# Cross attention: the sums of one key tile in eight go to an accumulator of their own, by an accumulating DMA

## What is computed

```
q = query @ Wq.T + bq; k = key @ Wk.T + bk; v = value @ Wv.T + bv      # 16 heads of 32
att = jnp.einsum('bhqd,bhkd->bhqk', q, k) / jnp.sqrt(jnp.float32(D_K))
att = jnp.where(mask == 0, -jnp.inf, att)
scores = jax.nn.softmax(att, axis=-1)
out = jnp.einsum('bhqk,bhkd->bhqd', scores, v)
```

## Time and profile before

| | us |
|---|---|
| median of 3 runs (3172.49 to 3174.4) | 3174.29 |
| the profiled execution, its own time | 3177.68 |
| its span, first to last instruction | 3175.9 |
| PE busy, all stages | 3039.1 (96%) |
| DVE busy | 1824.3 (57%) |
| ACT busy | 1346.5 (42%) |
| POOL busy | 43.9 (1%) |

### The profile page before, as it was taken

One profiled execution on the slowest core, in us unless ns is written; L12 is line 12 of the kernel. 1 busy time (PEld: TensorE's weight loads), 2 busy tenths in 40 slices (PEclk: granted clock), 3 DMA queues, 4 the chain that ended last, 5 costly groups with the idle time before them and its releaser, 6 DMA issues. The chain is left out here.

```text
span 3175.9 us, 45035 instructions
## 1 busy us (share of the span) xinstructions
PE 3039.1 (96%) x15853; PEld 1820.8 (57%) x15853; DVE 1824.3 (57%) x1578; ACT 1346.5 (42%) x1871; POOL 43.9 (1%) x38
## 2 busy tenths in 40 slices
PE   8999999998999999999999997979799899999998
PEld 4888888886333333333333333358344688888886
DVE  4444444444999999999999996047244111111111
ACT  3212121222988888888888882135100011111110
POOL 0000000000000000000000000000000200000000
PEclk9999999999999999999999998976899999999999
DMA  5555555555554555544554541000330678788774
GB/s 194 185 186 191 186 193 183 197 183 181 124 132 121 126 120 124 130 121 118 122 130 120 131 120 57 0 5 1 123 159 17 226 301 314 303 311 310 303 305 179
DMA packets 231254, 518.54 MB, mean 163 GB/s; under 512 B 20578, under 2 KB 86626, under 8 KB 201436
## 3 DMA queue, kind: packets, MB, share of 16 engines
q1 hardware_dynamic: 227564, 508.74, 49.7%
q0 software_dynamic: 3584, 8.39, 1.2%
HBM read 403.62 MB, written 113.44 MB: 163 GB/s over the span
## 5 line engine op out<-in xcount | busy, mean ns | idle before, releaser
L791 DVE TENSOR_TENSOR AC<-AC,PR 128x2048 f32<-128x2048 f32 x496 | 1093.5, 2278 | 7.2 <-ACT PR L754 7.2
L754 ACT ACTIVATE PR<-PS 128x1024 f32<-128x1024 f32 x1024 | 994.4, 1023 | 144.5 <-DVE AC L791 98.2
L665 PE MATMUL PS<-QS,KS 128*128 128x512 f32 x2048 | 645.0, 436 | 19.2 <-ACTq L763 9.0
L665 PEld LDWEIGHTS PS<-QS,KS 128*128 128x128 f32 x2048 | 321.0, 189 | 549.9 <-ACT PR L754 514.4
L712 PE MATMUL PS<-PR,VC 128*32 128x512 f32 x4096 | 547.3, 606 | 1.0 <-ACT PR L754 1.0
L1393 ACT ACTIVATE SE<-PS,GB 128x128 f32<-128x128 f32 x256 | 73.2, 368 | 630.7 <-PE PS L1349 630.7
L365 ACT ACTIVATE KH<-PS,bk_s 128x512 fp32r<-128x512 f32 x128 | 88.1, 688 | 561.4 <-PE PS L416 561.4
L276 DVE SCALAR_TENSOR_TENSOR KL<-PS,bk_s,KH 128x512 fp32r<-128x512 f32 x128 | 95.8, 750 | 274.6 <-ACT KH L365 274.6
L1349 PEld LDWEIGHTS PS<-XE,WG 128*128 128x128 f32 x2048 | 238.8, 193 | 23.7 <-issue 23.7
L1349 PE MATMUL PS<-XE,WG 128*128 128x128 f32 x2048 | 240.5, 276 | 0.8 <-issue 0.8
L1349 PE MATMUL PS<-XE,WU 128*128 128x128 f32 x2048 | 239.1, 275 | 0.0
(11 more groups left out here) (149 smaller groups left out, 2265.9 us busy)
## 6 DMA issues: line engine op xcount, KB each, us to landing
KS<-kh_d SPq DMA_DIRECT2D x256, 256.0 KB
WU<-in_up_w SPq DMA_DIRECT2D x64, 1024.0 KB, 4.8
WG<-in_gw SPq DMA_DIRECT2D x64, 1024.0 KB, 6.9
WD<-in_down_w SPq DMA_DIRECT2D x64, 1024.0 KB, 8.9
AT<-in_ctx SPq DMA_DIRECT2D x32, 1024.0 KB, 5.5
kh_d<-KH SPq DMA_DIRECT2D x32, 1024.0 KB, 4.4
kl_d<-KL SPq DMA_DIRECT2D x32, 1024.0 KB, 6.4
v_d<-VS SPq DMA_DIRECT2D x128, 256.0 KB, 3.0
```

The costliest lines, as they stand in the source:

```text
L665: m = pe.matmul(PS[:, 2 * slot + jj, :], KS[s][:, j, t * P:(t + 1) * P], QS[x_][:, j, :], start=True, stop=True)
L754: nc.scalar.activation(PR[t][:, 2 * hp:2 * hp + 2], PS[:, 2 * slot:2 * slot + 2, :], ACT.Exp, scale=SCALE).then_inc(s_exp, 1)
L791: v.tensor_tensor(a[:], a[:], PR[t][:], ALU.add).then_inc(s_acc, 1)
```

## The change

The tile `q = KT - 1` of a pair (first chunk, `t = 3`, buffer PR3) is no longer added by DVE. POOL issues a DMA from PR3 to a new accumulator `AP[x_]`: a plain copy in a group's first pair, and in the other seven a DMA with `accum_op=ALU.add`, which adds the 1 MB in PR3 to the 1 MB in AP. It waits for both exponentials of the tile, and for the DMA of the pair before. DVE skips the tile (its counts `ADDS` fall from 8 to 7 a pair); where `normal` stood behind that tile's add it stands in its place. ACT waits for the DMA, in place of DVE's sum, before it writes PR3 again in the pair's second chunk. PE's denominator reads three accumulators in place of two, 12 matmuls for 8. `s_step` is counted up and waited for by nobody.

```diff
--- before.py
+++ after.py
@@ -579,13 +579,14 @@
 
 
         s_wo = sem("output_weights_in")
-        s_s, s_exp, s_pv, s_acc, s_l, s_o, s_rec, s_norm = (sem(n) for n in (
-            "scores_ready", "exp_ready", "tile_values_added", "sums_added",
+        s_s, s_exp, s_pv, s_acc, s_pacc, s_step, s_l, s_o, s_rec, s_norm = (sem(n) for n in (
+            "scores_ready", "exp_ready", "tile_values_added", "sums_added", "dma_sums_added", "dma_sums_step",
             "denominator_ready", "output_copied", "reciprocal_ready", "output_normal"))
         UN = 2 * KT
         GU = NCH * UN
         GT = NCH * KT
-        ADDS = 2 * KT
+        PQ = KT - 1
+        ADDS = 2 * KT - 1
         KVB, QSB = 4 * 16, 4 * 16
         SLOTS, PAIRS = 3, NCH // 2
         GA = PAIRS * ADDS
@@ -600,6 +601,7 @@
             VC.append(sb("VC1", [P, KT, P]))
             PR = [sb(f"PR{i}", [P, J, SQ]) for i in range(KT)]
             AC = [[sb(f"AC{x}{h}", [P, J, SQ]) for h in range(2)] for x in range(2)]
+            AP = [sb(f"AP{x}", [P, J, SQ]) for x in range(2)]
             RC = sb("RC", [P, SQ])
 
             def all_groups(engine, group):
@@ -656,6 +658,23 @@
                 nc.gpsimd.memset(KS[1][3 * DH:P].bitcast(F32), 1.0).then_inc(s_row, 1)
                 nc.gpsimd.memset(QS[1][3 * DH:P].bitcast(F32), 0.0).then_inc(s_row, 1)
 
+                def group(bg, x_, rounds, head=False, tail=False):
+                    def pair(i, phase, first=False, last=False):
+                        pool.wait_ge(s_exp, (bg * NCH + i * 2) * UN + 2 * PQ + 1 + SLOTS + 1)
+                        if first:
+                            if not head:
+                                pool.wait_ge(s_norm, bg)
+                            pool.sem_inc(s_step, 1)
+                            nc.gpsimd.dma_start(AP[x_][:], PR[PQ][:]).then_inc(s_pacc, 16)
+                        else:
+                            pool.wait_ge(s_pacc, (bg * PAIRS + i) * 16)
+                            pool.sem_inc(s_step, 1)
+                            nc.gpsimd.dma_start(AP[x_][:], PR[PQ][:], accum_op=ALU.add).then_inc(s_pacc, 16)
+
+                    all_pairs(pool, pair)
+
+                all_groups(pool, group)
+
             @block.tensor
             def _(pe):
                 def scores(u, s, x_, slot):
@@ -674,9 +693,9 @@
                 def denominator(x_):
 
                     for j in range(J):
-                        for h in range(2):
-                            m = pe.matmul(PS[j * DH:(j + 1) * DH, SUMB, :], ones[:], AC[x_][h][:, j, :],
-                                          start=h == 0, stop=h == 1)
+                        for h, a in enumerate((*AC[x_], AP[x_])):
+                            m = pe.matmul(PS[j * DH:(j + 1) * DH, SUMB, :], ones[:], a[:, j, :],
+                                          start=h == 0, stop=h == 2)
                     m.then_inc(s_l, 1)
 
                 def group(bg, x_, rounds, head=False, tail=False):
@@ -714,6 +733,7 @@
                                 m.then_inc(s_pv, 1)
                                 if first and s == 0 and t == 2 and not head:
                                     pe.wait_ge(s_acc, bg * GA + ADDS)
+                                    pe.wait_ge(s_pacc, bg * (PAIRS * 16))
                                     pe.wait_ge(s_rec, bg)
                                     denominator(1 - x_)
 
@@ -728,6 +748,7 @@
                 pe.sem_inc(s_s, 2 * GU)
                 all_groups(pe, group)
                 pe.wait_ge(s_acc, BG * GA + ADDS)
+                pe.wait_ge(s_pacc, BG * (PAIRS * 16))
                 pe.wait_ge(s_rec, BG)
                 denominator(1)
 
@@ -747,10 +768,12 @@
                                 act.wait_ge(s_s, N * UN + 2 * GU + u + 1)
                                 if hp == 0:
                                     act.wait_ge(s_pv, N * KT + KT + t + 1)
-                                    if s == 1:
+                                    if s == 1 and t == PQ:
+                                        act.wait_ge(s_pacc, (bg * PAIRS + i) * 16 + 16)
+                                    elif s == 1:
                                         act.wait_ge(s_acc, (bg * PAIRS + i) * ADDS + ADDS + t + 1)
                                     else:
-                                        act.wait_ge(s_acc, (bg * PAIRS + i) * ADDS + KT + t + 1)
+                                        act.wait_ge(s_acc, (bg * PAIRS + i) * ADDS + KT - 1 + t + 1)
                                 nc.scalar.activation(PR[t][:, 2 * hp:2 * hp + 2], PS[:, 2 * slot:2 * slot + 2, :], ACT.Exp,
                                                      scale=SCALE).then_inc(s_exp, 1)
                                 if first and s == 0 and u == 1 and not head:
@@ -782,15 +805,18 @@
                             N = bg * NCH + i * 2 + s
                             for t in range(KT):
                                 q = s * KT + t
+                                if q == PQ:
+                                    if first and not head:
+                                        normal(bg - 1)
+                                    continue
+                                k = q if q < PQ else q - 1
                                 a = AC[x_][q % 2]
                                 dve.wait_ge(s_exp, N * UN + 2 * t + 1 + SLOTS + 1)
                                 if first and q < 2:
                                     v.tensor_copy(a[:], PR[t][:]).then_inc(s_acc, 1)
                                 else:
-                                    dve.wait_ge(s_acc, (bg * PAIRS + i) * ADDS + ADDS + q - 1)
+                                    dve.wait_ge(s_acc, (bg * PAIRS + i) * ADDS + ADDS + (k if q == PQ + 1 else k - 1))
                                     v.tensor_tensor(a[:], a[:], PR[t][:], ALU.add).then_inc(s_acc, 1)
-                                if first and q == KT - 1 and not head:
-                                    normal(bg - 1)
 
                     all_pairs(dve, pair)
 
```

## The result

| | us |
|---|---|
| before, median (3172.49 to 3174.40, 4 runs) | 3173.63 |
| after, median (3366.72 to 3381.39, 4 runs) | 3379.61 |
| ratio after to before | 1.0641 (1.0614 to 1.0667) |
| profiled execution after, span | 3377.5 |

The change makes the kernel 206 us slower; 3430 was forecast, with 3160 to 3740 as the range. The attention stage grew from 1141.6 us (first to last exponential) to 2132.3 - 783.7 = 1348.6 us, by 207, so all of it lies there.

What follows compares the result with a forecast made beforehand. DVE bounds the attention stage at 2.20 us a tile, PE 0.08 behind. 56 pairs x 22.1 = 1237.6, plus 135.7 and 28.2, make 1401.5 against 1141.6; less 3 at the end, +257 us: 3430, range 3160 to 3740.

Steps and rivals of the forecast that it cites:

- the conditions that were named for it: Attention stage: some 56 ACT waits of about 5 us, landing near 11 us, DVE idle ended by ACT, clock below 1.00.
- the forecast for a hidden DMA: Attention stage: the DMA lands below 7.7 us, so the whole gain of 31 us stands, 3143 us.
- L, issue to landing: Life of the 1 MB accumulating DMA: 2.7 fixed plus 8.3 by bytes, 11.0 us, range 8.0 to 15.7.
- ten exponentials, up to the next issue: ACT from one PR3 wait to the next: nine starts at 0.92 plus 1.02, 9.3 us.
- clock, a pair that loses it: PE idles 4.3 us, the granted clock falls to 0.50; 1.1 to 2.6 us lost a pair, 1.8 taken.
- by bytes 4 x 2.08 = 8.3: Engine time of the 1 MB accumulation, scaled from the 256 KB scatter into `out`: 8.3 us.
- two plain streams of 2.64 us: Low bound on the accumulation's engine time, two operands read at the price of plain 1 MB loads: 5.3 us.
- let longer rows and traffic cancel: DMA into AP: longer rows shorten it, other traffic adds 0 to 4.7 us; taken as cancelling, leaving 11.0.
- the deciding point: DMA landing at which the attention stage is neither faster nor slower: 56 x (L + 9.3) + 163.9 = 1144.6, L = 8.2 us.
- it fits: Rival for the DMA into AP: it lands early enough to be hidden, 3143 us below 7.7; chance 0.15.
- Rival 3, late descriptors,: POOL cannot write the DMA's descriptors while DVE adds: landing 13.3 us, +397, 3571 us; chance 0.1 of the 0.75.
- Rival 2,: Traffic doubles the DMA's landing to 21.5 us: +890, 4060 us; chance 0.07 for anything over 15.7.

Runs made afterwards that it cites:

- Taking out the wait alone: Changed kernel with a fifth exponential buffer for the tile that the DMA adds, so ACT meets the wait a whole pair later: 3169.70 us, ratio 0.9986.
- the kernel with both edits: Changed kernel with the fifth exponential buffer and the denominator matmuls run accumulator by accumulator: 3149.68 us, ratio 0.9924.
- copy: Changed kernel with all 64 DMAs into AP as plain copies, the adding left out: 3192.43 us, ratio 1.0054.
- tiny loads: Changed kernel with SP's key and value loads cut to a few KB from the second chunk pair on: 3200.49 us, ratio 1.0086.
- the reordering: Denominator matmuls accumulator by accumulator, not head by head: 3352.81 us on the changed kernel, 3149.68 us on it with a fifth exponential buffer.
- the kernel with the filled pause: Changed kernel with ten extra, unread PE matmuls before its wait in the six middle pairs of each group: 3336.55 us, ratio 1.0509.

## Why the prediction came out as it did

**Right:** the sign and the mechanism, and most of the conditions that were named for it. ACT waits 56 times for the DMA, DVE's idle time is ended by ACT, the granted clock is 0.93 over the stage, and the mean of the score matmuls rose from 436 ns, in the page's groups of before, to 448. The landing (9.1 us for near 11) and each wait (3.5 for about 5) were shorter than named. Taking out the wait alone gives back all of it, and the forecast for a hidden DMA (3143) came within 7 us of the kernel with both edits (3150).

**The terms:**

| term | forecast | measured |
|---|---|---|
| fixed part of the DMA, issue and landing | 2.7 | 1.7 |
| 16 engines' time to move and add 1 MB | 8.3 (low end 5.3) | 5.2 |
| other traffic | 0 (0 to 4.7) | 2.2 |
| L, issue to landing | 11.0 | 9.1 |
| ten exponentials, up to the next issue | 9.3 | 10.4 |
| clock, a pair that loses it | 1.8 | 1.4 |
| a group's denominators | 2.9 | 5.3 |

*Mis-sized: the adding.* The step "by bytes 4 x 2.08 = 8.3" took the scatter's price for a DMA with rows four times as long and SBUF at both ends. The low end, two plain streams of 2.64 us, is what the quiet DMA costs: 5.2, against 2.7 for a quiet copy, so adding costs twice a copy here and not three times. The step "let longer rows and traffic cancel" then hid a real 2.2 us of traffic under a term that was 3 too large. The L of the sum was 1.9 us too long, 56 x 1.9 = 106 us. The Trainium skill's page "DMA: Bandwidth & Descriptors", section "Anatomy of one DMA — SWDGE (gpsimd) path", would give 4.4 us for 1 MB. The quiet plain copy agrees with it, at 4.6 us (4.5 to 4.8); beside the loads the copy lands in 6.9, and the accumulation in 6.9 quiet and 9.1 beside them, so the fit was no price for this DMA. The first pairs' copies, taken as under 6.5, landed in 6.7 to 7.9; ACT wanted PR3 back only some 10.7 us after their issue, so nothing hung on it.

*Left out: POOL's way to the issue.* The cycle was counted from exponential to exponential. In the trace the tenth exponential after a restart ends at 1339.63 + 1.02 = 1340.65 and POOL issues at 1341.32, 0.67 us later. Nine exponentials take 8.50, a pitch a little above 0.92, and the tenth waits 0.18 for PE, so 9.7 to its end, and the stretch is 10.4 us without loss of clock. This is why the deciding point was wrong: "L = 8.2" rests on L + 9.3. With L + 10.4, 22.0 for each first pair and 13 for the two long edges, 56 x (L + 10.4) + 8 x 22.0 + 13 is 1144.6 at L = 6.7, an estimate. The runs agree with it: with landings of 6.9 (copy, tiny loads) the kernel is 0.5% and 0.9% slower than before, where the prediction would have called both faster. The chance of 0.15 for "it fits" was thus too large.

*Left out: the order of the denominators.* 2.4 us a group, 19 us in all; the reordering gave 27 in the median in one kernel, 20 in the other, and 2.7 us a group in the trace.

*Almost right for a wrong reason: the clock.* It was to fall behind a pause of 4.3 us. With the shorter L PE's pause was mostly 1.4 to 2.4 us, 1.83 in the pair shown, and it fell in 47 of 55 pairs all the same; 1.4 us were lost in 34 of them, more in others. The kernel with the filled pause shows that this is the clock.

Sum of these against the forecast: -106 for L, +62 for the stretch (1.1 x 56), -22 for the clock (0.4 x 56), +19 for the denominators: -47, so 3383. Measured 3380, which is closer than terms of this kind allow one to claim. It also shows that the forecast's nearness (51 us) is in part luck: an L that was 106 us too dear hid 81 us that were left out.

*Rival 3, late descriptors,* did not come: POOL's issue takes 842 to 919 ns, 0.67 us behind the exponential. In the changed kernel only 16 of the 56 issues fall beside a running DVE add. The kernel with tiny loads is the better witness: there 53 of 56 do, mostly with some 0.6 us of the add to go; the issues take 842 to 919 ns as well, and the landing is 7.0 in the median. The inference in the Trainium skill's page "SBUF — State Buffer", section "Who interferes with whom", that such adds spare the descriptor writing fits these numbers; descriptors were not timed by themselves. *Rival 2,* a doubled landing, did not come; the longest is 10.9.

## What to carry to other kernels

When work moves from an engine to a DMA, the question is not what the DMA costs but when its buffer is wanted back; a DMA of 9 us is free with 17 us of room and costs 210 us, in 56 waits, with 6 (3379.61 us against 3169.70). Count the whole cycle from one issue to the next, with the issuing engine's own delay in it, before naming a break-even, and look how near the next engine stands: here the relief of DVE was worth some 1%, since PE was 0.08 us a tile behind. Where one accumulator more goes into a chain of narrow matmuls, their order can cost more than their number.

## What the runs showed of the hardware that was not expected

- An accumulating DMA from SBUF to SBUF of 1 MB takes 5.2 us of all 16 engines, twice a plain copy's 2.7, and lands 6.9 us after POOL's issue with next to nothing beside it, a plain copy 4.6; 512 KB take 2.8 and 4.5. Beside the kernel's loads the two land in 9.1 and 6.9.
- Beside this DMA an SP load can suffer, too: over 1341 to 1350.5 us the values' load takes 7.7 us to landing. It is no rule: the median of these loads is 3.0 us, where it was 2.8 before, and the longest 9.6, where it was 7.0. Nobody waits for the values. Its row in the DMA view of the changed kernel over that stretch:

```profile
VC<-v_d SPq DMA_DIRECT2D x1, 256.0 KB, 7.7
```

- Twelve matmuls of 32 columns take 5.3 us if three in a row go to the same 32 columns, and 2.7 if four different ones alternate. Eight with two in a row took 1.94, and ten, half of the heads with three and half with two, 3.6.
- How long PE paused did not tell whether the granted clock fell. It fell after a pause of PE of 1.83 us (with short waits around it), shorter than the pauses of 3.2 and 3.56 us behind which it fell in the trace before, and even after one of 1.38. Yet in eight pairs it stayed at 1.00, behind pauses of 1.36 to 2.42 us. So no threshold for the pause follows from these traces; in the kernel whose pauses were filled with matmuls it stayed up. PE's timeline with the shortest and the longest pause that left it at 1.00, each with a windows' row around it, all of the changed kernel:

```profile
1332.03 0.73 PE L684 MATMUL PS<-QS,KS 128*128 128x512 f32 x2 [1.36 <-ACT PR L777]
...
1322.00:1333.00 11.00, 9.46 (x55) 3.68 (x51) 9.57 (x5) 7.65 (x9) 0.86 (x1) 1.00 1.04 238
...
1165.43 0.73 PE L684 MATMUL PS<-QS,KS 128*128 128x512 f32 x2 [2.42 <-ACT PR L777]
...
1155.00:1174.00 19.00, 16.39 (x95) 6.08 (x93) 16.49 (x9) 14.40 (x17) 0.70 (x1) 1.00 0.69 155
```
